# State-space block and attention on one core: input projection by channel block in 512 columns, halo rows apart, new orders, LayerNorm shift from PSUM

## The chip, the cores and the metric

The program runs on one core of a Trainium2 chip. Its engines work side by side, each through its own queue in order: PE (TensorE, matmuls and transposes), ACT (ScalarE), DVE (VectorE), POOL (GpSimd), and SP, which issues the DMAs. They wait for each other through semaphores. The metric is the device time of one execution in microseconds, the median of several; lower is better.

## The reference

Input x is (4, 64, 64, 256) in fp32. Layer 0, cut to its lines:

```python
x_norm = _layernorm(x, norm_g, norm_b)
xz = x_norm @ in_proj_W                       # 256 -> 2 x 384
x_proj, z = (xz[..., :INNER], xz[..., INNER:])
windows = _window_partition(x_proj, WS)       # 2 x 2 windows: sequences of 4 tokens
y_fwd = _light_s6(windows, fwd_...)           # proj; dt = silu(..); state = exp(dt*a)*state + dt*b*x; y = state.c
y_bwd = jnp.flip(_light_s6(jnp.flip(windows, 1), bwd_...), 1)     # 8 states per channel and direction
y_ssm = _window_unpartition(0.5 * (y_fwd + y_bwd), WS, h, w, b)
y_dw = depthwise 3x3 convolution of x_proj, padding 'SAME'
y_conv = jax.nn.gelu(y_dw @ pw_W, approximate=False)
y = alpha * y_ssm + (1.0 - alpha) * y_conv
x_out = shortcut + y * jax.nn.silu(z) @ out_W
h2 = _layernorm(x_out, norm2_g, norm2_b)
return x_out + jax.nn.gelu(h2 @ fuse_W1 + fuse_b1, approximate=False) @ fuse_W2 + fuse_b2
```

Layer 1 is self-attention over the 4096 pixels of each image, with 32-channel queries and keys. The change doesn't touch it.

## The kernel before, in words

Layer 0 goes over 32 tiles of 512 tokens (8 image rows of 64). A tile k has a front (LayerNorm, input projection, dt, x by token, the gates), a middle (16 chains, 8 states in 2 directions, over 4 tokens) and a back (mixing, output projection, second LayerNorm, fuse, keys, queries and values for layer 1). An iteration of the loop runs the middle of tile k, the back of k - 1 (steps with `-`), the front of k + 1 (steps with `+`), and conv, pw and z of tile k. The order on each engine is written out by hand in `PE_ORDER`, `ACT_ORDER`, `DVE_ORDER` and `POOL_ORDER`. Steps that the prediction names:

- `xnt0/1`, `xnth`: PE turns the normalized x to channels first; `xnth` turns the two halo rows (above and below the tile). `xnt` holds for each half (dr, even or odd rows) 256 tokens and 64 halo columns.
- `inx0` to `inx5`: input projection of channel block cb = i // 2 and half dr = i % 2: 2 matmuls of 320 columns (L489; each matmul is two passes in the profile, each with a weight load), then three copies on ACT: `x_ch` (L686), the padded image `xp` (L691), and the halo row of xp (L694).
- `proj`, `dtf0` to `dtf3`, `dtb0` to `dtb3`: dt of token t, forward and backward; a pair is issued together in the `dtb` step (L534, L538) and copied by ACT with silu (L717) to `dt`. `xk0` to `xk2`: x by token, `x_win` (L733). `bct`: gates b and c.
- `argq` (POOL, L828) multiplies dt with the rates of chain q; `expq` (ACT, L782, L783) takes its exponents; `stN` (DVE) is a third of a slot of the recurrence; `accq` (POOL, L841) adds the chain's last output; `umf`/`umb` (POOL, L819) make u = dt * x_win.
- `yt`, `out0/1`, `ln2_stats/mean/std/shift/norm`, `h2t`, `w10` to `w21`, `x1t0/1`, `fg0` (keys and queries), `v0/1` (values): the back. `ln2_shift` and `ln1_shift` are L880, -mean / std for 4 or 5 rows of tokens.
- `conv0a` waits for conv's bank and input; the 108 small matmuls are issued in `conv2a`, `conv0b` and `conv2c`. `z0` to `z2` project the gate. `ow` scales two tokens of y.

Results of front steps go in turn through three PSUM banks (`psF`, `BANK_OF`), those of the back through two (`psB`), states through three (`psS`, columns 0 to 383). A PE step waits until the former user of its bank is copied. ACT loads a table (L651, 1.28 us) when it changes between exp, silu and gelu: ten times in a tile.

SP waits for `w21` and stores the residual; then waits for `fg0`, stores keys and queries in six DMAs, loads the next `xb` in four, and stores the values behind `v0` and `v1`.

## Time and profile before

| what | value |
|---|---|
| median of 3 runs | 4567.81 us (4566.51 to 4570.78) |
| profiled execution | 4575.34 us |
| its span on the core | 4573.5 us |
| granted TensorE clock over the span | 0.983 |
| layer 0 (about 0 to 2612 us), layer 1 (2612 to the end) | 32 tiles; 32 chunks of queries |

Times in the rows are microseconds from the start of the span. A timeline row has: start, length (of all that it merges), engine, line, operation, out<-in with shapes, count, and in brackets the engine's idle time before it and who ended it. The length of one instruction includes a tail that overlaps the next instruction on its engine, so the pace is read from starts. PEclk is the granted clock as a share of full speed. An engine whose idle time is short is near its limit, but what bounds a loop of engines is the chain that has no spare wait in it.

### The profile page before, as it was taken

What the parts mean: (1) busy time and instruction counts of PE and PEld (TensorE: products, weight loads), DVE (VectorE), ACT (ScalarE), POOL (GpSimd) and SP (SyncE); (2) the same over time, 40 slices, a digit from 0 to 9 for tenths busy, and PEclk for the clock granted to TensorE, in tenths of its full rate; (3) what the DMA queues carried; (4) which work ended last, traced back from release to release, by engine and by line L of the source; (5) the groups of instructions that cost most, each with busy time, mean ns of one, the idle gap of its engine ahead of it and who ended that gap; (6) DMA issues with size and microseconds to landing.
All of it is one profiled execution on the core that took longest, in us unless ns stands there. A gap on an engine that the chain in (4) does not pass through costs nothing. (4 is left out here: it accounts for less than half of the span.)

```text
span 4573.5 us, 78801 instructions
## 1 busy us (share of the span) xinstructions
...
## 2 busy tenths in 40 slices
...
DMA packets 139073, 194.82 MB, mean 43 GB/s; under 512 B 18428, under 2 KB 106470, under 8 KB 138726
## 3 DMA queue, kind: packets, MB, share of 16 engines
...
q8 instruction: 166, 2.72, 0.2%
...
## 5 line engine op out<-in xcount | busy, mean ns | idle before, releaser
L1423 POOL TENSOR_TENSOR pl<-probs,ph 128x512 fp32r<-128x512 f32 x1024 | 1318.7, 1289 | 543.9 <-PE ps_o L1527 269.0
L828 POOL TENSOR_TENSOR dec<-dt,rates 128x384 f32<-128x384 f32 x1536 | 1493.1, 1003 | 253.9 <-ACT dt L717 198.3
L1626 ACT ACTIVATE ph<-ps_s 128x512 fp32r<-128x512 f32 x1024 | 613.3, 599 | 773.3 <-PE ps_s L1510 768.7
L1639 DVE TENSOR_REDUCE part_max<-ps_m 128x1 f32<-128x512 f32 x992 | 667.3, 688 | 343.8 <-PE ps_m L1495 343.5
L1519 PE MATMUL ps_o<-ph,values_high 128*128 128x512 f32 x2048 | 809.1, 395 | 0.1
L1519 PE MATMUL ps_o<-ph,values_low 128*128 128x512 f32 x2048 | 804.4, 393 | 0.0
L1669 DVE TENSOR_TENSOR ps_a<-probs,ps_a 128x512 f32<-128x512 f32 x992 | 682.1, 688 | 48.0 <-ACT probs L1628 40.4
L1527 PE MATMUL ps_o<-pl,values_high 128*128 128x512 f32 x2048 | 634.4, 391 | 0.0
L1628 ACT ACTIVATE probs<-ps_s 128x512 f32<-128x512 f32 x1024 | 609.5, 595 | 0.0
L986 DVE SCALAR_TENSOR_TENSOR psS<-u,bc,psS 128x384 f32<-128x384 f32 x1024 | 597.1, 615 | 1.2
L995 DVE SCALAR_TENSOR_TENSOR y_tok<-psS,bc,y_tok 128x384 f32<-128x384 f32 x960 | 554.7, 608 | 4.5
L841 POOL TENSOR_TENSOR y_tok<-y_tok,dec 128x384 f32<-128x384 f32 x512 | 512.5, 1001 | 20.1 <-DVE dec L976 14.0
L782 ACT ACTIVATE psS<-dec 128x384 f32<-128x384 f32 x512 | 256.1, 500 | 351.8 <-POOL dec L828 327.4
L962 DVE SCALAR_TENSOR_TENSOR psS<-u,bc,psS 128x384 f32<-128x384 f32 x512 | 314.0, 613 | 202.2 <-ACT psS L782 200.3
L489 PE MATMUL psF<-xnt,in_w 128*128 128x320 f32 (+1 forms) x1152 | 438.2, 510 | 14.7 <-ACT xp L694 12.5
L1519 PEld LDWEIGHTS ps_o<-ph,values_high 128*128 128x128 f32 x2048 | 388.2, 190 | 92.1 <-DVE o_ch L1674 0.5
L1519 PEld LDWEIGHTS ps_o<-ph,values_low 128*128 128x128 f32 x2048 | 388.1, 190 | 86.1
L1527 PEld LDWEIGHTS ps_o<-pl,values_high 128*128 128x128 f32 x2048 | 384.9, 188 | 87.3
L783 ACT ACTIVATE dec<-dec 128x768 f32<-128x768 f32 x512 | 428.8, 838 | 0.0
L651 ACT ACT_TABLE_LOAD x319 | 409.3, 1283 | 5.6
L489 PEld LDWEIGHTS psF<-xnt,in_w 128*128 128x128 f32 x1152 | 218.7, 199 | 177.9 <-issue 114.3
L510 PE MATMUL psF<-xp,conv_w 32*32 32x512 f32 x6912 | 269.8, 594 | 32.1 <-ACT q_sb L722 32.1
...
## 6 DMA issues: line engine op xcount, KB each, us to landing
...
xf<-in_x_dram SPq DMA_DIRECT2D x128, 128.0 KB
xb<-in_x_dram SPq DMA_DIRECT2D x128, 128.0 KB
...
out_dram<-res SPq DMA_DIRECT2D x128, 128.0 KB
```

Of the source, the lines that this page charges most:

```text
L489: mm = pe.matmul(outs, wts[:, kb, :], src[:, kb], start=kb == 0, stop=kb == KB - 1)
L828: last = nc.gpsimd.tensor_tensor(dec[:, q % RING, j - 1, :], dt[:, par, d, token_of(d, j), :], rates[:, d, n, :], ALU.mult)
L841: nc.gpsimd.tensor_tensor(y_tok[:, par, t, :], y_tok[:, par, t, :], dec[:, q % RING, T - 2, :], ALU.add).then_inc(acc_ok, 1)
L986: nc.vector.scalar_tensor_tensor(s_t, u[:, d, t, :], scalar(q, t, "b"), s_t, ALU.mult, ALU.add).then_inc(state_ok, 1)
L995: nc.vector.scalar_tensor_tensor(y_t, s_t, scalar(q, t, "c"), y_t, ALU.mult, ALU.add).then_inc(state_ok, 1)
L1423: nc.gpsimd.tensor_tensor(pl[:, m % DEPTH, :], probs[:, m % DEPTH, :], ph[:, m % DEPTH, :].bitcast(F32), ALU.subtract).then_inc(pl_ok, 1)
L1519: mm = pe.matmul(ps_o[cb][:, :], v[:, m, cb * P:(cb + 1) * P], ph[:, m % DEPTH, :], start=m == 0 and v is vh, stop=False)
L1527: pe.matmul(ps_o[cb][:, :], vh[:, m, cb * P:(cb + 1) * P], pl[:, m % DEPTH, :], start=False, stop=m == KEYS - 1).then_inc(lo_done[cb], 1)
L1626: nc.scalar.activation(ph[:, m % DEPTH, :], ps_s[m % 2][:, :], ACT.Exp).then_inc(ph_ok, 1)
L1628: nc.scalar.activation(probs[:, m % DEPTH, :], ps_s[m % 2][:, :], ACT.Exp).then_inc(probs_ok, 1)
L1639: nc.vector.tensor_reduce(part_max[:, qt, kc:kc + 1], ps_m[r % 2][:, :], AX.X, ALU.max).then_inc(max_out, 1)
L1669: nc.vector.tensor_tensor(ps_a[:, :], probs[:, m % DEPTH, :], ps_a[:, :], ALU.add).then_inc(acc_ok, 1)
```

## The change

The input projection of x is done by whole channel block: `inx0` to `inx2`, each 2 matmuls of 512 columns, one `x_ch` copy and two `xp` copies. The lower halo row of the three blocks is one step `inh` with 6 matmuls of 64 columns (two per block) and three copies; the upper halo row is copied by ACT from the last row of the tile before, which lies in the other half of `xp`, in one instruction for the three blocks. The orders are new. `ln1_shift` and `ln2_shift` copy the mean into unused columns of a state bank in PSUM, wait for that copy, and read it from there. With 29 front jobs in place of 32, banks go round by three throughout.

```diff
 PE_ORDER = """
-    z0 z1 yt0- yt1- yt2- z2 out0- conv0a out1- conv1a conv2a conv0b conv0c conv1c conv2c xnt0+ h2t0- h2t1- xnt1+
+    z0 z1 yt0- yt1- yt2- z2 out0- out1- conv0a conv1a conv2a conv0b conv0c conv1c conv2c xnt0+ h2t0- h2t1- xnt1+ pw0
...
-BANK_OF = {step: (i % FRONT_BANKS if i < len(FRONT_JOBS) - len(FRONT_JOBS) % FRONT_BANKS else 1)
-           for i, step in enumerate(jobs(True, (0, 1), True))}
+BANK_OF = {step: i % FRONT_BANKS for i, step in enumerate(jobs(True, (0, 1), True))}
...
+                if job == "inh":
+                    for cb in range(CB):
+                        for kb in range(KB):
+                            mm = pe.matmul(bank[:, cb * W:(cb + 1) * W], in_w[:, kb, cb * P:(cb + 1) * P],
+                                           xnt[:, kb, 1, TOK // 2:], start=kb == 0, stop=kb == KB - 1)
...
-                    if kind == "inx":
-                        cb, dr = int(i) // 2, int(i) % 2
-                        outs, src = bank[:, 0:TOK // 2 + W], xnt[:, :, dr, :]
-                        wts = in_w[:, :, cb * P:(cb + 1) * P]
...
+                    outs = bank[:, :].rearrange("p (h n) -> p h n", h=2)
+                    src = xnt[:, :, :, 0:TOK // 2]
+                    c0 = (INNER if kind == "z" else 0) + int(i or 0) * P
+                    wts = xproj_w if kind == "proj" else in_w[:, :, c0:c0 + P]
...
                 elif kind == "v":
+                    if i == 0:
+                        pe.wait_ge(back_act, emptied(g, "x1t1")[1])
...
-                    cb, dr = int(job[-1]) // 2, int(job[-1]) % 2
-                    nc.scalar.activation(x_ch[:, cb, dr * 256:(dr + 1) * 256], bank[:, 0:TOK // 2], ACT.Identity,
+                    cb = int(job[-1])
+                    nc.scalar.activation(x_ch[:, cb, :], bank[:, :], ACT.Identity,
                                          scale=mix[:, 0, cb:cb + 1], bias=mixed_bias[:, cb:cb + 1])
...
+                    for dr in range(2):
+                        dst = xp[:, par, cb, 1 + dr:dr + ROWS:2, 1:W + 1].rearrange("p wr (wc dc) -> p dc wr wc", dc=2)
+                        last = nc.scalar.activation(dst, bank[:, dr * 256:(dr + 1) * 256].rearrange(
+                            "p (dc wr wc) -> p dc wr wc", dc=2, wr=ROWS // 2), ACT.Identity, bias=in_bias[:, cb:cb + 1])
+                elif job == "inh":
+                    if not (exact(f) and f == 0):
+                        act.wait_ge(front_out, front_job(f - 1, "inx2"))
+                    nc.scalar.activation(xp[:, par, :, 0, 1:W + 1], xp[:, 1 - par, :, ROWS, 1:W + 1], ACT.Copy,
+                                         scale=edge[:, bass.ds(2 * f, 1)])
+                    for cb in range(CB):
+                        last = nc.scalar.activation(xp[:, par, cb, ROWS + 1, 1:W + 1], bank[:, cb * W:(cb + 1) * W],
+                                                    ACT.Identity, scale=edge[:, bass.ds(2 * f + 1, 1)],
+                                                    bias=halo_bias[:, cb, bass.ds(2 * f + 1, 1)])
...
                     dve.wait_ge(ok, base + 2)
+                    mean = mv[:, :, 0:1]
+                    if own_bank is not None:
+                        mean = own_bank[:, INNER:INNER + n].rearrange("p (t s) -> p t s", s=1)
+                        nc.vector.tensor_copy(mean, mv[:, :, 0:1]).then_inc(mean_ok, 1)
+                        means.append(tile)
+                        dve.wait_ge(mean_ok, len(means))
                     dve.wait_ge(std_ok, tile + 1)
-                    last = nc.vector.scalar_tensor_tensor(shift[:, :, :], mv[:, :, 0:1], -1.0, std[:, :, :],
+                    last = nc.vector.scalar_tensor_tensor(shift[:, :, :], mean, -1.0, std[:, :, :],
```

In the order tables, ACT has `z2` ahead of `ln1_norm` and `xnth` ahead of `w10`; `fg0` stands behind the `xk` steps on PE and ACT and behind `st47` on DVE, `v0` where it stood; on DVE `out0`, `out1` and `ln2_shift` stand one `st` step earlier each; on POOL `acc0` and `acc5` change places with `umb0` and `umb3`, and `acc14` stands ahead of `umf3`.

PE from the second dt pair to the keys, queries and values; dt_w is the pair, xb the turns `x1t0` and `x1t1`, fg_w `fg0`, y_ch `xk`, value_w `v0`. Before:

```order
L534 MATMUL psF<-dt_w,proj_sb 128x384 x2
L538 MATMUL psF<-bias_row,two 128x384 x2
L489 MATMUL psF<-xnt,in_w 128x320 x2
L456 MATMUL psB<-ident,xb 128x128 x4
L534 MATMUL psF<-dt_w,proj_sb 128x384 x2
L538 MATMUL psF<-bias_row,two 128x384 x2
L456 MATMUL psB<-ident,xb 128x128 x4
L489 MATMUL psF<-xnt,in_w 128x320 x2
L534 MATMUL psF<-dt_w,proj_sb 128x384 x2
L538 MATMUL psF<-bias_row,two 128x384 x2
L609 MATMUL psB<-xt,fg_w 64x512 x2
L456 MATMUL psF<-ident,y_ch 128x128 x12
```

And now:

```order
L533 MATMUL psF<-dt_w,proj_sb 128x384 x2
L537 MATMUL psF<-bias_row,two 128x384 x2
L455 MATMUL psB<-ident,xb 128x128 x4
L533 MATMUL psF<-dt_w,proj_sb 128x384 x2
L537 MATMUL psF<-bias_row,two 128x384 x2
L470 MATMUL psF<-xnt,in_w 128x64 x6
L455 MATMUL psB<-ident,xb 128x128 x4
L533 MATMUL psF<-dt_w,proj_sb 128x384 x2
L537 MATMUL psF<-bias_row,two 128x384 x2
L616 MATMUL psB<-value_w,xt 128x256 x4
L455 MATMUL psF<-ident,y_ch 128x128 x12
L608 MATMUL psB<-xt,fg_w 64x512 x2
```

The projection between the first two dt pairs is gone, the one ahead of the last pair has become `inh` and stands ahead of `x1t1`, and `fg0` has changed places with `v0`.

ACT in the same place, from the second dt pair's copies on (y_ch is x_ch here, xt the copies of `x1t`). Before:

```order
L717 ACTIVATE dt<-psF 128x384 x2
L686 ACTIVATE y_ch<-psF,mixed_bias,mix 128x256
L691 ACTIVATE xp<-psF,in_bias 128x2x4x32
L694 ACTIVATE xp<-psF,halo_bias,edge 128x64
L766 ACTIVATE xt<-psB 128x512
L717 ACTIVATE dt<-psF 128x384 x2
L766 ACTIVATE xt<-psB 128x512
L686 ACTIVATE y_ch<-psF,mixed_bias,mix 128x256
L691 ACTIVATE xp<-psF,in_bias 128x2x4x32
L694 ACTIVATE xp<-psF,halo_bias,edge 128x64
L717 ACTIVATE dt<-psF 128x384 x2
```

And now:

```order
L724 ACTIVATE dt<-psF 128x384 x2
L773 ACTIVATE xt<-psB 128x512
L724 ACTIVATE dt<-psF 128x384 x2
L698 ACTIVATE xp<-xp,edge 128x3x64
L701 ACTIVATE xp<-psF,halo_bias,edge 128x64 x3
L773 ACTIVATE xt<-psB 128x512
```

Two half jobs of three copies each have gone from here, and the four copies of `inh` stand ahead of the second `xt` copy; the third dt pair's copies follow.

## Rows read from the trace of the kernel before

**Rows 1.** Windows: stretch, busy us (count) by engine, PEclk, DMA share, GB/s.
```profile
69.30:2406.70 2337.40, 2183.41 (x14206) 1375.58 (x14207) 2131.49 (x4364) 1905.41 (x3404) 2094.66 (x2161) 0.98 0.12 40
1236.75:1313.92 77.17, 72.73 (x481) 46.07 (x480) 71.28 (x147) 63.76 (x116) 69.83 (x73) 1.00 0.13 44
1313.92:1392.65 78.73, 74.37 (x481) 46.87 (x480) 71.28 (x147) 63.87 (x116) 69.84 (x73) 0.98 0.12 41
```
**Rows 2.** Source L660: duration ns min/median/max, first and last start us.
```profile
L660 ACT ACTIVATE std<-mv,eps x31: 283/284/288, 69.3 to 2406.7; 128x5 f32<-128x5 f32 x31
```
**Rows 3.** Windows ahead of and at the lower clock, second tile.
```profile
1370.00:1373.00 3.00, 1.43 (x10) 0.96 (x11) 3.00 (x7) 2.99 (x8) 1.90 (x2) 1.00 0.30 123
1373.10:1376.00 2.90, 2.90 (x8) 1.53 (x8) 1.88 (x4) 1.70 (x5) 0.00 (x0) 0.50 0.01 3
```
**Rows 4.** Timeline of PE: start us, length us, op, tiles, count.
```profile
1295.90 1.24 PE L489 MATMUL psF<-xnt,in_w 128*128 128x320 f32 x4
...
1373.11 2.34 PE L489 MATMUL psF<-xnt,in_w 128*128 128x320 f32 x4
```
**Rows 5.** Timeline of ACT in the tile from 1236.70.
```profile
1255.36 2.08 ACT L750 ACTIVATE hid<-xb,shift,std 128x256 f32<-128x256 f32 x4 [1.95 <-DVE shift L880]
...
1264.64 0.49 ACT L782 ACTIVATE psS<-dec 128x384 f32<-128x384 f32 x1 [0.99 <-POOL dec L828]
...
1273.63 0.49 ACT L782 ACTIVATE psS<-dec 128x384 f32<-128x384 f32 x1 [0.77 <-POOL dec L828]
...
1276.70 0.56 ACT L686 ACTIVATE y_ch<-psF,mixed_bias,mix 128x256 f32<-128x256 f32 x1
1277.14 0.51 ACT L691 ACTIVATE xp<-psF,in_bias 128x256 f32<-128x256 f32 x1
1277.52 0.41 ACT L694 ACTIVATE xp<-psF,halo_bias,edge 128x64 f32<-128x64 f32 x1
1277.80 0.71 ACT L763 ACTIVATE hid<-psB,col 128x512 f32<-128x512 f32 x1
...
1293.37 0.87 ACT L717 ACTIVATE dt<-psF 128x384 f32<-128x384 f32 x2
...
1295.70 0.91 ACT L717 ACTIVATE dt<-psF 128x384 f32<-128x384 f32 x2
...
1298.29 0.88 ACT L717 ACTIVATE dt<-psF 128x384 f32<-128x384 f32 x2
...
1302.22 1.54 ACT L733 ACTIVATE x_win<-psF 128x512 f32<-128x512 f32 x3
```
**Rows 6.** Timeline of POOL in the same tile.
```profile
1256.52 1.00 POOL L841 TENSOR_TENSOR y_tok<-y_tok,dec 128x384 f32<-128x384 f32 x1 [0.26 <-DVE dec L976]
...
1298.87 2.92 POOL L828 TENSOR_TENSOR dec<-dt,rates 128x384 f32<-128x384 f32 x3 [4.01 <-ACT dt L717]
...
1303.88 3.87 POOL L819 TENSOR_TENSOR u<-dt,x_win 128x384 f32<-128x384 f32 x4 [1.13 <-ACT x_win L733]
```
**Rows 7.** Timeline of PE in the same tile.
```profile
1248.31 8.35 PE L510 MATMUL psF<-xp,conv_w 32*32 32x512 f32 x216 [0.59 <-ACT q_sb L722]
1258.02 0.66 PE L456 MATMUL psF<-ident,xf 128*128 128x128 f32 x4 [1.36 <-ACT y_ch L707]
...
1290.96 1.34 PE L489 MATMUL psF<-xnt,in_w 128*128 128x320 f32 x4 [0.26 <-ACT xp L694]
...
1294.38 0.88 PE L534 MATMUL psF<-dt_w,proj_sb 48*128 48x384 f32 x3 [1.64 <-ACT dt L717]
...
1299.95 1.53 PE L456 MATMUL psF<-ident,y_ch 128*128 128x128 f32 x12
```
**Rows 8.** Timeline of DVE in the same tile.
```profile
1254.54 0.79 DVE L880 SCALAR_TENSOR_TENSOR shift<-mv,std 128x4 f32<-128x4 f32 x1
...
1301.01 0.62 DVE L962 SCALAR_TENSOR_TENSOR psS<-u,bc,psS 128x384 f32<-128x384 f32 x1 [3.21 <-ACT psS L782]
```
**Rows 9.** Source L1265, the same instruction in the setup.
```profile
L1265 DVE SCALAR_TENSOR_TENSOR shift<-mv,std x1: 166/166/166, 23.8 to 23.8; 128x5 f32<-128x5 f32 x1
```

More of the change, by code:

```diff
@@ L40 @@
 PE_ORDER = """
-    z0 z1 yt0- yt1- yt2- z2 out0- conv0a out1- conv1a conv2a conv0b conv0c conv1c conv2c xnt0+ h2t0- h2t1- xnt1+
-    pw0 w10- xnth+ pw1 w11- proj+ pw2 inx0+ w12- inx1+ w13- inx2+ dtf0+ dtb0+ w20- inx3+ w21- dtf1+ dtb1+ inx4+
-    x1t0- dtf2+ dtb2+ x1t1- inx5+ dtf3+ dtb3+ fg0- xk0+ xk1+ xk2+ v0- bct+ v1-
+    z0 z1 yt0- yt1- yt2- z2 out0- out1- conv0a conv1a conv2a conv0b conv0c conv1c conv2c xnt0+ h2t0- h2t1- xnt1+ pw0
+    w10- xnth+ pw1 w11- proj+ pw2 inx0+ w12- inx1+ w13- inx2+ dtf0+ dtb0+ w20- w21- dtf1+ dtb1+ x1t0- dtf2+ dtb2+
@@ L44 @@
+    inh+ x1t1- dtf3+ dtb3+ v0- xk0+ xk1+ xk2+ fg0- bct+ v1-
 """.split()
 ACT_ORDER = """
-    exp1 ln1_std+ exp2 ow exp3 z0 z1 ln1_norm+ z2 exp4 ln2_std- exp5 ln2_norm- conv0c conv1c conv2c xnt0+ exp6
-    h2t0- h2t1- xnt1+ exp7 exp8 pw0 w10- xnth+ pw1 w11- exp9 proj+ exp10 pw2 inx0+ w12- inx1+ w13- exp11 inx2+
-    exp12 dtf0+ dtb0+ exp13 inx3+ exp14 dtf1+ dtb1+ inx4+ x1t0- dtf2+ dtb2+ x1t1- inx5+ dtf3+ dtb3+ exp15 fg0-
-    xk0+ xk1+ xk2+ exp0+ v0- bct+ v1-
+    exp1 ln1_std+ exp2 ow exp3 z0 z1 z2 ln1_norm+ exp4 ln2_std- exp5 ln2_norm- conv0c conv1c conv2c xnt0+ exp6 h2t0-
@@ L50 @@
+    h2t1- xnt1+ exp7 exp8 pw0 xnth+ w10- pw1 w11- exp9 proj+ exp10 pw2 inx0+ w12- inx1+ w13- exp11 inx2+ exp12 dtf0+
+    dtb0+ exp13 exp14 dtf1+ dtb1+ x1t0- dtf2+ dtb2+ inh+ x1t1- dtf3+ dtb3+ exp15 v0- xk0+ xk1+ xk2+ exp0+ fg0- bct+
+    v1-
 """.split()
 DVE_ORDER = """
-    st0 ln1_stats+ st1 ln1_mean+ st2 yt0- st3 yt1- st4 st5 yt2- st6 ln1_shift+ st7 st8 st9 out0- st10
-    out1- ln2_stats- ln2_mean- st11 st12 st13 ln2_shift- st14 st15 st16 st17 st18 st19 st20 st21 st22
-    st23 st24 st25 st26 st27 st28 st29 st30 st31 st32 st33 st34 st35 st36 st37 st38 st39 w20- w21- st40 st41
@@ L55 @@
-    st42 st43 st44 st45 fg0- st46 st47 gd_mul+ v0- gd_sum+ v1-
+    st0 ln1_stats+ st1 ln1_mean+ st2 yt0- st3 yt1- st4 st5 yt2- st6 ln1_shift+ st7 st8 out0- st9 out1- st10
+    ln2_stats- st11 ln2_mean- st12 ln2_shift- st13 st14 st15 st16 st17 st18 st19 st20 st21 st22 st23 st24 st25 st26
+    st27 st28 st29 st30 st31 st32 st33 st34 st35 st36 st37 st38 st39 w20- w21- st40 st41 st42 st43 st44 st45 v0-
+    st46 st47 gd_mul+ fg0- gd_sum+ v1-
 """.split()
 POOL_ORDER = """
-    arg2 arg3 umb0 acc0 arg4 acc1 arg5 umb1 umb2 acc2 arg6 acc3 arg7 acc4 arg8 umb3 acc5 arg9 acc6 arg10 acc7
@@ L59 @@
-    arg11 acc8 arg12 acc9 arg13 acc10 arg14 acc11 arg15 acc12 arg0+ acc13 umf0+ umf1+ umf2+ umf3+ acc14 acc15
-    arg1+
+    arg2 arg3 acc0 umb0 arg4 acc1 arg5 umb1 umb2 acc2 arg6 acc3 arg7 acc4 arg8 acc5 umb3 arg9 acc6 arg10 acc7 arg11
+    acc8 arg12 acc9 arg13 acc10 arg14 acc11 arg15 acc12 arg0+ acc13 umf0+ umf1+ umf2+ acc14 umf3+ acc15 arg1+
 """.split()
@@ L458, in front @@
             def front(step, f, par):
-                kind, i = (step, "") if step in ("proj", "bct", "xnth") else (step[:-1], step[-1])
+                kind, i = (step, "") if step in ("proj", "bct", "xnth", "inh") else (step[:-1], step[-1])
                 job = step
```

35 lines of the change are left out of this document (14 added, 21 removed).

## The prediction

> **What bounds the kernel now.** The page has PE busiest, but it adds up two layers, and the change touches layer 0 alone. A window over layer 0, from 69.3 to 2406.7, has PE busy 2183 of 2337 us, DVE 2131, POOL 2095, ACT 1905 [rows 1]: four engines nearly full, so the sums don't name the bound. `std<-mv,eps` (step `ln1_std`) runs once a tile, 31 times from 69.3 to 2406.7 [rows 2]: a tile takes 2337.4/30 = 77.91 us on average.
>
> Two neighbouring tiles differ: 77.17 us at a granted clock of 1.00, then 78.73 us at 0.98 [rows 1]. A window in the second shows PEclk 0.50, the lower level (1.2 GHz); just before, PE had worked 1.43 us in 3.00 [rows 3]. Four passes of L489 that take 1.24 us in the first tile, at 1295.90, take 2.34 there [rows 4]. So a thin stretch of PE around `dtf2` costs 1.56 us in some tiles, and the mean gives their share: (77.91 - 77.17)/1.56 = 0.47.
>
> Then the timeline of the tile at full clock, 1236.70 to 1313.87 (all times below are in it), engine by engine, for what each waits for last.
> - ACT waits for POOL's exponents at 1264.64 (0.99) and last at 1273.63 (0.77, `exp10`). From there until it has copied `x_win` (three copies from 1302.22) its rows have no wait [rows 5].
> - POOL waits for ACT at 1298.87 (4.01, for `dt`) and at 1303.88 (1.13, for `x_win`). From there until `exp10`'s exponents of the next tile it waits once, 0.26 for DVE, at 1256.52 [rows 6].
>
> These two pieces close a loop: ACT from 1273.63 to 1303.88 is 30.25 us, POOL from 1303.88 to 1273.63 + 77.17 is 46.92; together 77.17, the whole period. PE's waits (0.59, 1.36, 1.64) are for ACT [rows 7], and DVE has 3.21 us spare at 1301.01 [rows 8]. So the bound is ACT's in-order queue from `exp10` to `xk2`, and POOL's 47 us behind it, and not PE.
>
> **The change, part by part.**
>
> *Input projection on ACT.* An `inx` job now goes from 1276.70 to 1277.80: 0.44 for the x_ch copy, 0.38 for xp, 0.28 for the halo, 1.10 in all, six times 6.60 [rows 5]. After: three jobs of one 512-column copy with scale and bias and two xp copies. The 512 columns cost between 0.48 (L733, plain, the pace of three in 1.54 with the tail off) and 0.88 (twice 0.44); I take the middle, 0.67. Three jobs: 3 x (0.67 + 0.76) = 4.29. `inh` adds three halo copies at 0.28 and one of 3 x 64 from SBUF, between 0.28 and 0.44, taken as 0.40: 1.24. Sum 5.53, **1.07 us less** for ACT in the loop (ends 0.3 and 1.7).
>
> *Input projection on PE.* Six times 1.24 = 7.44 now. By columns 3 x 512 stand against 6 x 320: 5.95. The 6 matmuls of 64 columns have 12 passes with a weight load each; nearest are the 12 turns of L456 at 1299.95, 1.53 us [rows 7]; by columns alone they would be 0.5. With 1.5 PE's work stays the same; the edit can pay only through ACT.
>
> *How much of ACT's saving arrives.* Up to `dtf1` there are four half jobs now (4.40) and three full ones after (4.29): 0.1 us; `exp13` and `exp14` now stand together, and the table loads are as many. So dtf1's copy starts near 1293.2 (now 1293.37). PE's 1.64 us wait to 1294.38 ends when both copies are done; after the change `dtf2` and `dtb2` lie in the banks of `dtb0` and `dtf1`, and PE can start near 1293.8. By its rows PE then needs about 1.1 us for the pair, 1.4 for `inh`, 0.5 for `x1t1`, 1.1 for the next pair: ready at 1294.9, 1296.2, 1296.7 and 1297.8. ACT waits for it: dtf2/dtb2 to 1295.7 (two copies, some 0.8), `inh` 1296.2 to 1297.5, `x1t1` to 1298.0, then dtf3, whose copy now starts at 1298.29 [rows 5]. That is 0.3 us earlier, and 0.6 if the 512 columns take less than I count. `v0` stands ahead of `xk0` where `fg0` was, one 512-column copy for another. I take **0.55 us** for the loop (ends 0 and 1.2).
>
> *POOL.* `acc14` ahead of `umf3` moves one addition; nothing is added. It delays DVE's `st0` of the next tile, which needs all four u, by one addition at most, and DVE comes to `st0` only behind `st47`, `gd_mul`, `fg0`, `gd_sum` and `v1`. The 0.26 wait at 1256.52 should go, since DVE's queue gets there sooner (next two items): **0.2 us** (ends 0 and 0.26).
>
> *LayerNorm shift.* L880 on 4 elements takes 0.79 us; the same instruction on 5 elements took 0.166 in the setup (L1265), before POOL's loop ran [rows 8, 9]. After: a copy to PSUM and a product from it, at 0.166 each with a wait between, about 0.4. Twice a tile DVE saves 0.4; if either waits as L880 does, nothing. The Trainium skill ("SBUF — State Buffer", two separate sides) has a pair of ports that GpSimd and a Vector instruction with two SBUF inputs take in turn, each for its whole length; by that rule one input in PSUM frees L880, and the 0.166 agrees. Either way it lies beside DVE's 3.21 us.
>
> *`out1` ahead of `conv0a`, `z2` ahead of `ln1_norm`.* PE's wait at 1248.31 (0.59) goes, and the one before `out1`. `ln2_shift` stands one piece of `states` earlier, about 1 us, so `ln2_norm` can start about 1.1 us before 1255.36, and with it the conv copies and PE's 1258.02. The wait of 1.36 there stays, as conv ends that much earlier too. What is late next: ACT meets POOL's exponents at 1264.64, and will wait 2.1 in place of 0.99. **Nothing**, with POOL's pace as the cover; without it, 1.1 us.
>
> *SP.* `fg0` is emptied some 4 us later on DVE, and behind it on SP stand six stores of keys and queries, four `xb` loads and the two v stores. `xb` is read by `out0`, behind `st8` of the next tile; no wait of now is for it, and I count nothing (upper end: 1 us a tile, in rival 2).
>
> At full clock: 77.17 - 0.55 - 0.2 = 76.42.
>
> **The clock.** Now PE runs `inx4` at 1290.96 after a wait of 0.26, `x1t0`, then idles 1.64 [rows 7]: 1.9 us idle. After, `inx4` is gone. dtf1/dtb1 end near 1290.8, `x1t0` waits for DVE's `w21`, which stands where it stood, until about 1292.1, and PE idles again until 1293.8: about 2.5 us idle. So I expect the lower clock in more tiles, 0.7 of them (ends: 0.2, as a shorter period shifts where tiles fall, and 1). Its price stays at 1.56, since it falls on dtf2, `inh` and dtf3, for which ACT waits.
>
> A mean tile: 76.42 + 0.7 x 1.56 = 77.51, 0.40 less than 77.91; times 31 tiles, **12 us**. The profiled execution took 4575.3, 1.8 more than its span and 7.5 more than the median of the runs shown; against that median, 4567.8, the forecast is **4555**.
>
> **Rivals.**
> 1. *The lower clock in every tile.* 76.42 + 1.56 = 77.98, 2 us slower in all: 4570. For it: 2.5 us idle in place of 1.9. Against: half of the tiles with 1.9 kept the full clock. The Trainium skill ("TensorE: Matmul & The Clock Gate", what's actually happening) says that the low level is the default and activity lifts it; by that rule thinning this stretch counts against the change. Chance 0.15.
> 2. *Slower: `inh` is too long.* It stands ahead of `x1t1` and `dtf3` with a turn of its own on PE and four copies on ACT, where ACT already waits for PE. If it costs ACT 0.8 us more than I count, the loop gains nothing, and that is where this case begins to decide. At 1.2 more: 77.4 at full clock, with 0.9 of the tiles slowed 78.8, 0.9 x 31 = 28 us slower: 4596; 4580 halfway. Against: no 64-column copy exceeds 0.41. Chance 0.13.
> 3. *The thin stretch costs less often*: share 0.2. 76.42 + 0.31 = 76.73, 1.18 x 31 = 37 us: 4531. For it: the share now rests on where a tile's 1.9 us fall, and the period changes that. Chance 0.22.
> 4. *POOL's pace holds*: no gain in the loop, share as now: 4568. Against: POOL waits 4.01 and 1.13 for ACT. Chance 0.08.
>
> The forecast, share 0.5 to 0.9 and 0.4 to 1.4 off the full-clock tile, gives 4543 to 4563: chance 0.42.
>
> **Numbers.** 0.2% (9 us) is about what a measurement of this kernel can tell from no change. Faster: rival 3 (0.22) and most of the forecast (0.36): 0.58. Same: the rest of it, rival 4, and most of rival 1: 0.25. Slower: rival 2 and a little of rival 1: 0.17. The range 4525 to 4577 reaches to rivals 3 and 1; the likeliest case's own is 4543 to 4563.
>
> **What would show it.** `std<-mv,eps` about 76.4 us apart in tiles at full clock; ACT's wait for POOL at `exp8` near 2 us; a copy and a product of some 0.16 each for the shift; no wait ahead of conv; PEclk below 1.00 in about 20 of 30 tiles, near dtf2. It is wrong if full-clock tiles still take 77.2 (the loop was another one), or if the count of slowed tiles is far from 20.

## The result

| | before | after |
|---|---|---|
| median, runs on the same chip | 4569.30 us (4566.51 to 4572.12) | 4612.41 us (4611.31 to 4613.47) |
| span of the profiled execution | 4573.5 us | 4609.6 us |
| granted clock over the span | 0.983 | 0.963 |

The change makes the kernel slower: the ratio after to before is 1.0093, 95% interval 1.0081 to 1.0105. The forecast was 4555, with 4577 as its upper end.

The windows of the kernel after, over layer 0 and over one tile, answer to [rows 1] (stretch, then busy us and count of PE, PE's weight loads, DVE, ACT and POOL, then the granted clock, the DMA share and GB/s).

```profile
72.60:2439.90 2367.30, 2250.21 (x14200) 1402.90 (x14201) 2107.10 (x4422) 1870.42 (x3254) 2094.13 (x2161) 0.94 0.12 39
1254.96:1333.59 78.63, 75.55 (x480) 47.23 (x479) 70.43 (x149) 62.54 (x110) 69.84 (x73) 0.96 0.12 40
```

The step `ln1_std` and the two instructions of the shift, each by its source line (duration in ns), answer to [rows 2, 9].

```profile
L661 ACT ACTIVATE std<-mv,eps x31: 282/284/286, 72.6 to 2439.9; 128x5 f32<-128x5 f32 x31
...
L895 DVE SCALAR_TENSOR_TENSOR shift<-psS,std x62: 160/164/166, 77.7 to 2537.3; 128x5 f32<-128x5 f32 x31, 128x4 f32<-128x4 f32 x31
...
L891 DVE COPY psS<-mv x62: 153/157/159, 77.5 to 2537.1; 128x5 f32<-128x5 f32 x31, 128x4 f32<-128x4 f32 x31
```

A tile takes (2439.9 - 72.6)/30 = 78.91 us against 77.91, so 1.00 x 30 = 30 of the 36 us are in the loop. DVE, ACT and POOL are busy for less time or as much as before; PE alone is busy for longer, 2250 us against 2183 [rows 1], at a lower clock: PEclk 0.94 against 0.98. The trace's record of the granted clock has 28 of the 29 tiles behind the first at the lower level for a while (14 before), 222 us in all (48 before), and always from around `dtf2` and `inh` on. This is PE there (start, length, line, operation, out<-in, count, idle time ahead):

```profile
1308.19 0.92 PE L533 MATMUL psF<-dt_w,proj_sb 48*128 48x384 f32 x4
...
1310.58 0.63 PE L455 MATMUL psB<-ident,xb 128*128 128x128 f32 x4 [1.29 <-DVE xb L946]
1311.91 0.88 PE L533 MATMUL psF<-dt_w,proj_sb 48*128 48x384 f32 x3 [0.71 <-ACT dt L724]
...
1312.94 2.51 PE L470 MATMUL psF<-xnt,in_w 128*128 128x64 f32 x12
1315.24 1.06 PE L455 MATMUL psB<-ident,xb 128*128 128x128 f32 x4
1316.23 1.65 PE L533 MATMUL psF<-dt_w,proj_sb 48*128 48x384 f32 x4
...
1318.13 2.97 PE L616 MATMUL psB<-value_w,xt 128*128 128x256 f32 x8
```

and the windows of PE ahead of and inside the stretch:

```profile
1308.00:1311.50 3.50, 1.91 (x12) 0.91 (x10) 3.50 (x8) 3.47 (x6) 3.36 (x5) 1.00 0.07 27
...
1311.50:1312.90 1.40, 0.98 (x6) 0.55 (x6) 1.40 (x3) 1.14 (x3) 0.96 (x2) 1.00 0.75 307
1312.90:1315.20 2.30, 2.30 (x14) 2.27 (x13) 2.30 (x6) 0.87 (x2) 0.78 (x1) 0.59 0.01 4
...
1316.20:1322.00 5.80, 5.80 (x25) 4.21 (x25) 1.46 (x3) 4.84 (x10) 3.19 (x4) 0.66 0.00 0
```

The projection `inx4` is gone from ahead of `x1t0`, which waits 1.29 us for DVE (`w21`); `dtf2` waits 0.71 for ScalarE's dt copies. The clock is full until 1312.90 and falls right behind the start of `inh`: the window from 1312.90 to 1315.20, which `inh` fills, has 0.59, and the trace's record of the clock has the lower level (1.2 GHz) from 1313.31 to 1320.14. So what drew it in this tile stands ahead of `inh`, but for its first 0.37 us: the two idles, with the thin work around them, four turns of 128 columns and a dt pair of 48 rows. In 23 of the 28 tiles the fall lies inside `inh`'s twelve passes. All that follows is slow: `inh` takes 2.51, `x1t1` 1.06, and the four passes of the dt pair 1.65 where those of the pair ahead took 0.92 at 1308.19.

ACT and POOL of the same tile, and of the only tile behind the first that ran wholly at the full clock (229.28 to 306.37), answer to [rows 5, 6]. First ACT:

```profile
266.54 0.49 ACT L789 ACTIVATE psS<-dec 128x384 f32<-128x384 f32 x1 [0.59 <-POOL dec L835]
...
287.81 0.87 ACT L724 ACTIVATE dt<-psF 128x384 f32<-128x384 f32 x2 [0.40 <-PE psF L537]
289.29 0.46 ACT L698 ACTIVATE xp<-xp,edge 128x192 f32<-128x192 f32 x1 [0.61 <-PE psF L470]
...
1282.97 0.49 ACT L789 ACTIVATE psS<-dec 128x384 f32<-128x384 f32 x1 [1.77 <-POOL dec L835]
...
1294.84 0.77 ACT L687 ACTIVATE y_ch<-psF,mixed_bias,mix 128x512 f32<-128x512 f32 x1
1295.50 0.89 ACT L693 ACTIVATE xp<-psF,in_bias 128x256 f32<-128x256 f32 x2
...
1313.04 0.87 ACT L724 ACTIVATE dt<-psF 128x384 f32<-128x384 f32 x2 [0.40 <-PE psF L537]
1315.48 0.46 ACT L698 ACTIVATE xp<-xp,edge 128x192 f32<-128x192 f32 x1 [1.57 <-PE psF L470]
1315.85 0.98 ACT L701 ACTIVATE xp<-psF,halo_bias,edge 128x64 f32<-128x64 f32 x3
1316.72 0.60 ACT L773 ACTIVATE xt<-psB 128x512 f32<-128x512 f32 x1
1318.24 0.87 ACT L724 ACTIVATE dt<-psF 128x384 f32<-128x384 f32 x2 [0.93 <-PE psF L537]
```

Then POOL:

```profile
291.58 2.92 POOL L835 TENSOR_TENSOR dec<-dt,rates 128x384 f32<-128x384 f32 x3 [3.13 <-ACT dt L724]
...
296.54 2.93 POOL L826 TENSOR_TENSOR u<-dt,x_win 128x384 f32<-128x384 f32 x3 [1.08 <-ACT x_win L740]
...
1318.81 2.92 POOL L835 TENSOR_TENSOR dec<-dt,rates 128x384 f32<-128x384 f32 x3 [5.13 <-ACT dt L724]
...
1323.76 2.93 POOL L826 TENSOR_TENSOR u<-dt,x_win 128x384 f32<-128x384 f32 x3 [1.07 <-ACT x_win L740]
```

POOL waits 3.13 us for `dt` in the full-clock tile and 5.13 in the slowed one: there the lower clock reaches the loop. ACT's waits for PE ahead of `inh` and of the last dt pair are 1.57 and 0.93 there; at full clock the first is 0.61 and the second doesn't appear.

### The profile page after: what moved, and what is told of

Same layout as the page of the kernel before. It is cut to its first block and busy times, and to the rows that moved or that the text cites. A ratio compares the mean times of both kernels' runs of the same rounds, so it can differ in the third digit from the quotient of the medians.

```text
span 4609.6 us, 78766 instructions
## 1 busy us (share of the span) xinstructions
PE 4416.4 (96%) x24000; PEld 3128.3 (68%) x24000; DVE 3727.3 (81%) x7231; ACT 3158.7 (69%) x5620; POOL 3650.5 (79%) x3475
## 3 DMA queue, kind: packets, MB, share of 16 engines
q8 instruction: 166, 2.72, 0.2%
## 5 line engine op out<-in xcount | busy, mean ns | idle before, releaser
L835 POOL TENSOR_TENSOR dec<-dt,rates 128x384 f32<-128x384 f32 x1536 | 1493.4, 1004 | 265.7 <-ACT dt L724 219.5
L848 POOL TENSOR_TENSOR y_tok<-y_tok,dec 128x384 f32<-128x384 f32 x512 | 514.4, 1005 | 41.7 <-DVE dec L991 37.3
L488 PE MATMUL psF<-xnt,in_w 128*128 128x512 f32 x768 | 356.6, 594 | 0.9 <-ACT bc L710 0.7
L997 DVE TENSOR_TENSOR psS<-psS,dec 128x384 f32<-128x384 f32 x512 | 283.3, 553 | 1.1
L826 POOL TENSOR_TENSOR u<-dt,x_win 128x384 f32<-128x384 f32 x256 | 253.5, 1008 | 38.3 <-ACT x_win L740 38.3
```

Source lines behind the costliest of these rows:

```text
L835: last = nc.gpsimd.tensor_tensor(dec[:, q % RING, j - 1, :], dt[:, par, d, token_of(d, j), :], rates[:, d, n, :], ALU.mult)
L848: nc.gpsimd.tensor_tensor(y_tok[:, par, t, :], y_tok[:, par, t, :], dec[:, q % RING, T - 2, :], ALU.add).then_inc(acc_ok, 1)
```

## The experiments

In the kernels with fill in their name PE runs extra matmuls into a bank that is free at that moment, and nobody reads their results: they take away idle time of PE and put wide work in its place. Each measured time is a median; the ratio behind it, with its 95% interval, is to the kernel before run beside it (medians of 4569.3 to 4572.6 us, so a difference of two kernels that were not run together is good to some 3 us). Slowed tiles are counted behind the first, 29 in all; in the first the clock is low for 34 to 44 us in every kernel.

### Is it the clock, and is it the idle time?

**after_fill**: the kernel after, with extra matmuls in both idles.

```diff
+            def busy_work(bank, widths, free, n):
+                pe.wait_ge(free, n)
+                for cols in widths:
+                    pe.matmul(bank[:, 0:cols], w1[:, 0, 0:P], w1[:, 1, 0:cols], start=True, stop=True)
...
+                    if part == "all" and step == "x1t0":
+                        busy_work(psF[front_bank(tile, "dtf2")], (512, 256), front_out, bank_user_before(k + 1, "dtf2")[0])
+                    if part == "all" and step == "dtf2":
+                        busy_work(psB[BACK_JOBS.index("x1t1") % BACK_BANKS], (384,), back_dve, emptied(k - 1, "w21")[1])
```

> The changed kernel plus matmuls whose result nobody reads, where PE stands idle: 512 and 256 columns ahead of x1t0, 384 ahead of dtf2. Theory A (the loss is TensorE's lower clock, drawn by the thin stretch there, with tiles of 77.1 us at full clock): PEclk 1.00 in nearly all tiles, a mean tile of 77.1 to 77.3 in place of 78.9, so 50 us less than the changed kernel, about 4560. Theory B (the loss is the path of inh through PE and ACT): the added work can only cost, 4612 or more.

Measured: 4523.84 us, ratio 0.9892 (0.9875 to 0.9908). More work, and 89 us less than the kernel after, where 50 were expected. PE in the same stretch, the extra matmuls being L623:

```profile
1270.19 1.56 PE L623 MATMUL psF<-w 128*128 128x512 f32 x4
1271.59 0.60 PE L455 MATMUL psB<-ident,xb 128*128 128x128 f32 x4
1272.02 0.81 PE L623 MATMUL psB<-w 128*128 128x384 f32 x2
1272.90 0.88 PE L533 MATMUL psF<-dt_w,proj_sb 48*128 48x384 f32 x3
...
1273.92 1.55 PE L470 MATMUL psF<-xnt,in_w 128*128 128x64 f32 x12
...
1277.48 1.97 PE L616 MATMUL psB<-value_w,xt 128*128 128x256 f32 x8 [0.55 <-ACT xt L782]
```

`inh` takes 1.55 in place of 2.51, no tile behind the first is slowed, and a tile takes 76.19 us on average. So the lower clock costs the kernel after 78.91 - 76.19 = 2.72 us a tile, 82 us in 30. The 77.1 that the expectation took for a full-clock tile was too long: the one such tile stands behind a slowed one.

**after_fill_gap1** (only the first `busy_work`) and **after_fill_gap2** (only the second) ask which idle it is.

> The changed kernel with only the first filler, 512 and 256 columns in the 1.29 us wait ahead of x1t0; the 0.71 us ahead of dtf2 stays empty. Theory A1 (it is the sum of idle time and thin work around dtf2 that draws the lower clock, and 0.7 us idle is less than the 1.36 us that never drew it elsewhere): full clock in nearly all tiles, 4524 to 4532. Theory A2 (thin work by itself is enough: x1t0, dt with 48 rows, inh with 64 columns, x1t1): slowed tiles remain, 4550 or more.

> The changed kernel with only the second filler, 384 columns in the 0.71 us ahead of dtf2; 1.29 us stay idle ahead of x1t0. The first filler alone gave 4528. Theory A1 (idle time summed over the stretch decides; 1.29 is less than the 1.36 that draws nothing ahead of xnt0): full clock mostly, 4525 to 4545. Theory A2 (thin work counts as little as none, so 1.29 idle between it is too much): slowed tiles in half or more, 4560 or more.

Measured: 4527.71 (0.9898; 0.9881 to 0.9914) and 4529.4 (0.9907; 0.9890 to 0.9923), no slowed tile in either. Either idle alone (0.70 or 1.29 us) leaves the full clock; the two together don't. The extra matmuls are wide work as well as less idle time, and these runs don't tell the two apart.

**before_fill**: the same in the kernel before, 512 and 384 columns ahead of `dtf2`.

> The kernel before with matmuls of 512 and 384 columns, read by nobody, in the 1.64 us wait ahead of dtf2. Theory A: the 14 slowed tiles of 78.7 become 77.2, 22 us less than before, about 4547, PEclk 1.00 over layer 0. Theory B says nothing of the clock: 4568 or more, since work is added.

Measured: 4549.80 (0.9950; 0.9933 to 0.9966), tiles of 77.20, none slowed. The kernel before, too, pays (77.91 - 77.20) x 30 = 21 us for its clock.

**before_thin**: the kernel before with `inx4` ahead of `dtf1` on PE and ACT, which takes away the work between `dtb1` and `x1t0` as the change does; on ACT its copies now stand ahead of `dtf1`'s.

```diff
-    dtf0+ dtb0+ w20- inx3+ w21- dtf1+ dtb1+ inx4+ x1t0- dtf2+ dtb2+ x1t1- inx5+ dtf3+ dtb3+
+    dtf0+ dtb0+ w20- inx3+ w21- inx4+ dtf1+ dtb1+ x1t0- dtf2+ dtb2+ x1t1- inx5+ dtf3+ dtb3+
```

> The kernel before with nothing changed but inx4's place on PE and ACT: ahead of dtf1 in place of behind dtb1, so that x1t0's stretch is as empty as in the changed kernel. Theory A: the share of slowed tiles goes from 0.47 to 0.8 or more, 4585 to 4610. Theory B (clock follows from inh, or from nothing in this stretch): within 8 us of before.

Measured: 4644.18 (1.0157; 1.0140 to 1.0173), every tile slowed, where 4585 to 4610 was expected. One moved step in the old kernel costs 73 us. PE there:

```profile
1328.72 0.66 PE L456 MATMUL psB<-ident,xb 128*128 128x128 f32 x4
1331.77 1.65 PE L534 MATMUL psF<-dt_w,proj_sb 48*128 48x384 f32 x4 [2.39 <-ACT dt L717]
...
1334.58 2.34 PE L489 MATMUL psF<-xnt,in_w 128*128 128x320 f32 x4
```

The wait ahead of `dtf2` is 2.39 us, and `inx5` takes the 2.34 of [rows 4] behind it. Not all of the 73 us is clock: behind the first two, its tiles alternate between about 79.5 us with 3.4 at the lower level and 80.9 with 6.8. By that slope a tile without it would take some 78.1 (an estimate), 0.9 over before_fill's 77.20. That part would be the move itself; no run of this kernel with extra matmuls shows it.

### Which part of the change does what

**proj_only**: the new projection alone, its jobs at the places of the old ones (`inx1` where `inx2` stood, `inx2` where `inx4` stood, `inh` where `inx5` stood), mean from SBUF. **proj_fill**: the same with 512 extra columns ahead of `dtf2`.

```diff
-    inx0+ w12- inx1+ w13- inx2+ dtf0+ dtb0+ w20- inx3+ w21- dtf1+ dtb1+ inx4+ x1t0- dtf2+ dtb2+ x1t1- inx5+ dtf3+
+    inx0+ w12- w13- inx1+ dtf0+ dtb0+ w20- w21- dtf1+ dtb1+ inx2+ x1t0- dtf2+ dtb2+ x1t1- inh+ dtf3+
```

> The new projection under the orders of before (inx1 and inx3 dropped, inx2 and inx4 become full jobs, inx5 becomes inh), mean from SBUF, no filler; with filler it took 4534 with tiles of 76.42. Theory A: one full job stands in the thin stretch, but the wait for dtf1's copy is longer and inh's thin work follows it; slowed tiles in half or more, each 1.5 to 2.3: 4560 to 4590. Theory D (the projection never draws the clock; the new orders did): 4534 to 4545.

> The new projection alone: orders of before with inx1, inx3 dropped, inx2 and inx4 become the second and third full job, inx5 becomes inh; mean from SBUF; a filler of 512 columns ahead of dtf2. To be read against before with filler, 4550 (tiles of 77.19). The step of the prediction (ACT's shorter copies shorten the loop by 0.55): tiles of 76.6, 4533. If the gain of the changed kernel came from orders and shift: 4548 to 4552. If inh blocks ACT: above 4555.

Measured: 4531.87 (0.9913; 0.9896 to 0.9929) and 4533.90 (0.9915; 0.9898 to 0.9931), both with tiles of 76.49 and none slowed. The projection alone is worth 77.20 - 76.49 = 0.71 us a tile at full clock, and it takes away the slowed tiles of before as well: the full job `inx2` stands ahead of `x1t0`, and the one idle left ahead of `dtf2` is 1.16. ACT, which comes sooner now, has a wait for POOL at `exp14` that the kernel before doesn't have:

```profile
1273.09 0.49 ACT L789 ACTIVATE psS<-dec 128x384 f32<-128x384 f32 x1 [0.46 <-POOL dec L835]
```

**before_psum** and **before_psum_fill**: the kernel before with the mean through PSUM, without and with the extra matmuls of before_fill.

> The kernel before with the mean copied to PSUM, no filler; with filler it took 4546, tiles of 76.87, against 77.19. Tiles at full clock of 76.9; the share of slowed tiles decides the rest: 0.47 as now gives 4560; 0.3 to 0.9 gives 4552 to 4580. If it comes out above 4572, a part of the changed kernel that only shortens DVE is a loss through the clock alone.

> The kernel before with the mean copied to PSUM and the filler ahead of dtf2, against before with filler alone, 4550. Theory C1, as predicted: DVE is shorter by 0.8 us a tile and nothing else moves, 4548 to 4552. Theory C2: the 0.26 us wait of POOL for DVE goes and later waits with it, 0.2 to 0.5 us a tile, 4534 to 4544.

Measured: 4570.80 (0.9999; 0.9989 to 1.0009) and 4546.05 (0.9938; 0.9921 to 0.9954). At full clock a tile is 0.30 shorter (76.90 against 77.20); without the extra matmuls 17 tiles are slowed in place of 14, and the gain is gone.

**after_sbuf**: the kernel after with the mean read from SBUF (`if False:` in place of `if own_bank is not None:`), and **after_sbuf_fill**, with both `busy_work` calls as well.

> The changed kernel with the LayerNorm mean read from SBUF again, no copy to PSUM. Theory A and B both: DVE has over 2 us spare a tile, so the time stays within 5 us of the changed kernel's 4612; L895's shift takes 0.79 us again. Theory C (DVE's queue is now in the loop, as POOL waits for it at acc0, 0.7 us): about 0.4 us a tile more, 4622 or more.

> The changed kernel with both fillers and the mean read from SBUF again, so that the shift is priced without the lower clock around dtf2. Theory C1 (the shift lies beside DVE's spare time at full clock; its 27 us were all clock): within 5 us of the 4524 with the shift from PSUM. Theory C2 (DVE's queue sets POOL's and ACT's waits in the new orders): full-clock tiles of 76.5 to 77.3 in place of 76.14, 4536 to 4560.

Measured: 4638.96 (1.0145; 1.0128 to 1.0162) and 4649.18 (1.0167; 1.0150 to 1.0184). The first fits only the third theory, and the second is 89 us or more above both. In the new orders the PSUM copy is worth 27 us, and 125 in the filled kernels. Rows of the filled one show how. DVE:

```profile
1282.11 3.38 DVE L904 SCALAR_TENSOR_TENSOR shift<-mv,std 128x5 f32<-128x5 f32 x1
...
1295.40 0.62 DVE L904 SCALAR_TENSOR_TENSOR shift<-mv,std 128x4 f32<-128x4 f32 x1
```

POOL at the same time:

```profile
1281.61 0.99 POOL L835 TENSOR_TENSOR u<-dt,x_win 128x384 f32<-128x384 f32 x1
1282.57 2.90 POOL L844 TENSOR_TENSOR dec<-dt,rates 128x384 f32<-128x384 f32 x3
1287.74 1.00 POOL L857 TENSOR_TENSOR y_tok<-y_tok,dec 128x384 f32<-128x384 f32 x1 [2.27 <-DVE dec L1000]
```

and PE behind it:

```profile
1298.73 1.11 PE L455 MATMUL psF<-ident,xf 128*128 128x128 f32 x4 [3.60 <-ACT y_ch L723]
```

`ln1_shift` from SBUF takes 3.38 us and ends just as POOL's four back-to-back products (from 1281.61 to 1285.47) do; POOL itself then waits 2.27 for DVE, `ln2` is late, and PE idles 3.60 ahead of `xnt0`. Every tile falls to the lower clock behind that idle, and the extra matmuls around `dtf2` can't help. How much of the 125 us is this clock and how much the delay itself wasn't separated. With the mean in PSUM the same instruction takes 160 to 166 ns in all of its 62 runs. The Trainium skill ("SBUF — State Buffer", two separate sides) says that of a GpSimd instruction and a Vector instruction with two SBUF inputs, the one that starts first holds a shared pair of ports for its whole length, and the other waits. The trace agrees that the product with two SBUF inputs waits and the one with an input in PSUM doesn't; but the wait here covered POOL's whole run of instructions, not one. A run doesn't always shut it out: `ln2_shift`, in the middle of three back-to-back products (1295.00 to 1297.91), is through in 0.62. And in after_sbuf `ln1_shift` takes 0.15 or 0.16 in 18 of its 31 runs, as at 402.12, where it starts just as POOL goes from one instruction to the next, and 3.25 to 4.48 in 12:

```profile
402.12 0.16 DVE L895 SCALAR_TENSOR_TENSOR shift<-mv,std 128x5 f32<-128x5 f32 x1
```

So where the product meets POOL decides; what lets it in stays open.

**proj_psum**: projection and PSUM copy, all in the old orders.

> The kernel before with the new input projection and the PSUM copy of the mean, everything else in the old places, and no added matmuls. Theory A (the new orders let the lower clock in, the two other parts are gains that add up): full-clock tiles of 76.42 less about 0.3, that is 76.1, no tile slowed, since the thin stretch keeps its one idle of about 1.2 us; about 4523 us. Rival (part of the 76.14 of the filled kernel after belongs to the new orders): 76.4 and 4530 us. A second rival: the earlier end of the LayerNorm gives the stretch ahead of the delta weights another wait, and some tiles fall to the lower clock: 4535 to 4560.

Measured: 4525.90 (0.9898; 0.9881 to 0.9914), no slowed tile, 76.24 on average. Two parts of the change alone give what the filled kernel after gives (4523.84), without extra matmuls.

### Which move of the orders

**after_inx2_late**: `inx2` behind `dtb1` on PE and ACT. **after_inh_late**: `inh` (the halo matmuls; its expectation below calls them a transpose) behind `dtb3` on both.

```diff
-    inx0+ w12- inx1+ w13- inx2+ dtf0+ dtb0+ w20- w21- dtf1+ dtb1+ x1t0- dtf2+ dtb2+ inh+ x1t1- dtf3+ dtb3+
+    inx0+ w12- inx1+ w13- dtf0+ dtb0+ w20- w21- dtf1+ dtb1+ inx2+ x1t0- dtf2+ dtb2+ inh+ x1t1- dtf3+ dtb3+
...
+    inx0+ w12- inx1+ w13- inx2+ dtf0+ dtb0+ w20- w21- dtf1+ dtb1+ x1t0- dtf2+ dtb2+ x1t1- dtf3+ dtb3+ inh+
```

> The changed kernel with inx2 moved on PE and ACT from ahead of dtf0 to behind dtb1: 1.7 us of the kernel's own work in the thin stretch. Theory A: fewer tiles at the lower clock (under 20 of 30) and for a shorter time in each, a mean tile near 77.7, 4570 to 4585. Theory B: inh is where it was, so no more than 10 us change from 4612, or slower, as inx2's copies now stand ahead of dtf2's on ACT.

> The kernel after with only the transpose of the current tile's inh moved back behind the transposes of B, on TensorE and ScalarE, so that less thin work stands between the two idles. Theory A (the lower clock is drawn by idle time and thin work together, and inh's matmuls with their 0.4 to 0.6 us of wait make the stretch twice as long as before): the low spell is short again and in fewer tiles, 4570 to 4595 us. Rival (only the two idles of 1.3 and 0.7 us count): 27 or more of 30 tiles slowed as before, 4605 to 4620 us. Rival that ends lower still: with inh gone the second idle is closed too, no slow tile, 4525 us.

Measured: 4600.89 (1.0065; 1.0049 to 1.0082), 21 tiles slowed, and 4600.62 (1.0061; 1.0045 to 1.0078), 15 slowed but for some 10 us each (154 us in all). Each gives back only 12 us; the idles of 1.28 and 0.71 stay in the second, and in the first 0.84 and 0.72. after_inx2_late comes nearest to theory B. For after_inh_late no expectation was right: fewer slowed tiles, with longer stays.

**after_stretch_old**: all moves from `inx0` to `v1` taken back on PE, ACT and DVE, the other moves kept. **proj_psum_stretch_new**: the converse, only those moves made in proj_psum.

> The kernel after, with the input projection's jobs, inh, fg0 and v0 back in their old places on TensorE, ScalarE and VectorE (everything from inx0 to v1), the other moves of the new orders (out1, z2, xnth, ln2_shift, the additions and umb/umf on GpSimd) kept. Theory A (the stretch around dtf2 alone lets the lower clock in, the other moves are neutral): no slowed tile, full-clock tiles of 76.1 to 76.2, 4520 to 4530 us. Rival (another of the moves, such as the earlier ln2_shift or acc0 ahead of umb0, makes or shares the cause): part or all of the loss stays, 4560 to 4612 us.

> The converse: the new projection and the PSUM copy in the old orders, with only the part from inx0 to v1 of the new orders on TensorE, ScalarE and VectorE. Theory A: the whole loss of the kernel after, 25 or more of 30 tiles slowed, 4600 to 4620 us. Rival (the other moves are needed too): between 4526 and 4590 us.

Measured: 4540.17 (0.9929; 0.9912 to 0.9945) and 4619.51 (1.0101; 1.0085 to 1.0118). From both sides the stretch holds the loss: 72 us gained where it is undone, 94 lost where it alone is done, with 21 tiles slowed (25 or more were expected). But 12 tiles of after_stretch_old are still slowed, behind one idle of 1.53, where none was expected. Of its others, those behind a full-clock tile take 75.6 us, less than in any kernel so far; those behind a slowed one take some 76.2.

**after_stretch_old_fill** (512 extra columns ahead of `dtf2`) and **after_stretch_inh_first** (no extra matmuls, `inh` moved ahead of `dtf2` on PE and ACT) go on from there.

> The kernel with the new projection, the PSUM copy and the new orders outside the stretch (full-clock tiles of 75.60, 13 of 30 tiles slowed, 4540 us), plus one matmul of 512 columns, whose result nobody reads, in its idle of 1.5 us ahead of dtf2. Theory A (idle and thin work there draw the lower clock, and cost nothing else): all tiles at 75.6, about 4508 us. Rival (the filler only moves the low clock elsewhere, or delays dtf2): 4525 or more.

> The same kernel without a filler, inh moved ahead of dtf2 on TensorE and ScalarE, so that real work stands in the idle. Theory A: the idle ahead of inh shrinks to about 1.1 us, as it waits for one dt copy and not two, near the 1.16 at which the kernel with the projection alone kept the full clock; dtf2 comes 1 us later, dtf3 at the same time; no slowed tile, 75.6 to 76.0, 4508 to 4522 us. Rival (ScalarE is held by the four copies of inh ahead of the dt copies, so the loop grows): full-clock tiles of 76.3 or more, 4530. Second rival (thin work brought forward counts as idle does): still ten or more slowed tiles, 4535 to 4560.

Measured: 4512.45 (0.9868; 0.9852 to 0.9885), all tiles at 75.67 on average, the fastest of all; and 4557.09 (0.9964; 0.9952 to 0.9977), 19 tiles slowed and 76.6 to 76.7 at full clock. Real work in the idle didn't do: two idles are left, with the thin `inh` between them, and at full clock the loop is 1.0 longer:

```profile
1287.19 1.55 PE L470 MATMUL psF<-xnt,in_w 128*128 128x64 f32 x12 [1.05 <-ACT dt L724]
1289.10 1.31 PE L533 MATMUL psF<-dt_w,proj_sb 48*128 48x384 f32 x4 [0.35 <-ACT xp L693]
```

The last 0.57 us, from proj_psum's 76.24 to 75.67, are nearly all on POOL: from its first `u` of a tile to its last addition ahead of the wait for `dt` it needs 1274.07 - 1207.39 = 66.68 in proj_psum and 1264.31 - 1198.15 = 66.16 in after_stretch_old_fill. In proj_psum `acc0` (L848) stands between `umb0` (L826) and the next chain's product (L835):

```profile
1207.39 3.88 POOL L826 TENSOR_TENSOR u<-dt,x_win 128x384 f32<-128x384 f32 x4 [1.15 <-ACT x_win L740]
...
1221.91 1.00 POOL L826 TENSOR_TENSOR u<-dt,x_win 128x384 f32<-128x384 f32 x1
1222.87 1.00 POOL L848 TENSOR_TENSOR y_tok<-y_tok,dec 128x384 f32<-128x384 f32 x1
1224.02 2.92 POOL L835 TENSOR_TENSOR dec<-dt,rates 128x384 f32<-128x384 f32 x3
...
1274.07 1.01 POOL L848 TENSOR_TENSOR y_tok<-y_tok,dec 128x384 f32<-128x384 f32 x1
```

In after_stretch_old_fill, with POOL's new order, `acc0` (L855) comes first, then `umb0` (L833), then the product (L842):

```profile
1198.15 2.91 POOL L833 TENSOR_TENSOR u<-dt,x_win 128x384 f32<-128x384 f32 x3 [1.13 <-ACT x_win L747]
...
1212.53 1.00 POOL L855 TENSOR_TENSOR y_tok<-y_tok,dec 128x384 f32<-128x384 f32 x1
1213.48 1.01 POOL L833 TENSOR_TENSOR u<-dt,x_win 128x384 f32<-128x384 f32 x1
1214.44 2.93 POOL L842 TENSOR_TENSOR dec<-dt,rates 128x384 f32<-128x384 f32 x3
...
1264.31 1.01 POOL L855 TENSOR_TENSOR y_tok<-y_tok,dec 128x384 f32<-128x384 f32 x1
```

From the first of the pair to the product it is 2.11 us in the old order and 1.91 in the new: a product right behind an addition starts 1.15 after it (but for the one behind `acc15`, 0.95), and nearly all other pairs of POOL's instructions follow each other in 0.96. The new order takes away two such places (`acc0`, `acc5`), 0.2 each, and with `acc14` ahead of `umf3` the first six instructions take 1203.90 - 1198.15 = 5.75 in place of 1213.27 - 1207.39 = 5.88. No run moves the additions alone, so this rests on the rows.

## Why the prediction was wrong, step by step

Tile by tile the means add up (30 tiles):

| step | us a tile | from |
|---|---|---|
| before, filled | 77.20 | before_fill |
| new projection | -0.71 | proj_only |
| mean through PSUM | -0.25 | proj_psum |
| orders outside the stretch | -0.57 | after_stretch_old_fill |
| orders from `inx0` to `v1` | +0.52 | after_fill |
| lower clock of after | +2.72 | after |
| after | 78.91 | |

The clock of before is +0.71 on 77.20.

- **The bound** was right for the kernel before: ACT's queue from `exp10` to the last `x_win`, then POOL. In proj_psum the same cut gives 1283.54 - 1254.03 = 29.51 and 46.65, in sum the 76.16 of that tile; before they were 30.25 and 46.92. But ACT now waits 0.46 us for POOL at `exp14`, so what ACT saves ahead of it doesn't all count any more.
- **Input projection on ACT, and how much of it arrives**: forecast 1.07 and 0.55; measured 0.71 a tile with the projection alone (the 1.07 less the wait of 0.46 at `exp14` would be 0.61). The copies cost what was counted: 0.66 for 512 columns (1294.84 to 1295.50, counted 0.67), 1.24 for the four of `inh` (1315.48 to 1316.72, counted 1.24). In the new stretch ACT then waits 0.40 and 0.61 for PE, and its piece is 296.54 - 266.54 = 30.00, against 30.25 before and 29.51 in the old orders: 0.25 arrives. That ACT would wait for PE there was foreseen; the wait was counted 0.3 too small.
- **POOL**: forecast 0.2, since the wait at `acc0` would go. It went, by the PSUM copy: POOL waits 0.25 for DVE there in before_fill and proj_only, and not in before_psum or proj_psum. The swaps of `acc0` and `acc5` were left out without a reason and `acc14`'s was put at nothing; together they are worth about 0.5 on the very engine that bounds.
- **LayerNorm shift, beside DVE's spare time, worth nothing**: wrong. It is worth 0.25 to 0.30 a tile in the old orders, which is the very wait at `acc0` that the POOL item counts, so it didn't lie beside spare time; in the new orders it is worth 27 us in all. The step took L880's 0.79 as its price wherever it stood; in the new orders the product from SBUF can take 3.38.
- **`out1` ahead of `conv0a`**: the wait ahead of conv went and ACT waits 1.77 at `exp8` (forecast 2.1, [rows 5] had 0.99): right. PE's wait of 1.36 behind conv was to stay; it is 0.87.
- **At full clock 76.42**: measured 76.19 filled, and 77.09 in the only such tile of the kernel after, which stands behind a slowed one. That the sum came so near is luck in part: the gain that arrives from the projection in its new stretch was counted too high (0.55 against 0.71 - 0.52 = 0.19) and the orders outside it too low (nothing against 0.57), while the wait at `acc0` was right (0.2 against 0.25).
- **The clock** is the step that failed. The idle was forecast roughly (1.29 ahead of `x1t0` and 0.71 ahead of `dtf2`, 2.0 measured, "about 2.5" forecast), but what it draws was not. The step put the share at 0.7 and kept the price at 1.56, sum 1.09 a tile; it was 28 of 29 tiles and 2.72 a tile. The price of 1.56 was that of a short stay at the lower level (48/14 = 3.4 us a slowed tile in before); in after it is 222/28 = 7.9 us, so that `inh`, `x1t1`, the last dt pair and the values are all slow, and POOL gets `dt` 2.0 us late (5.13 against 3.13). Rival 1 had the share right and took the same price: 4570 in place of 4612. The sign hung on the price: 76.19 + 28/29 x 1.56 is 77.7, still under the 77.91 of before. Each us at the lower level cost 0.37 us after (82/222) and 0.44 before (21/48), so the length of the stays, not only their number, had to be in the sum. By the Trainium skill ("TensorE: Matmul & The Clock Gate", what's actually happening) the low level is the default and activity lifts it, which counts against thinning this stretch; that was noted there. The trace agrees, with 28 tiles in place of 14. The chance of 0.15 was too small.
- **Rival 2** ended nearer (4596), but for another reason: in the new stretch ACT loses 0.3 us more at full clock than was counted, not 1.2. Its sum has a slip as well: 76.42 + 1.2 is 77.6, not 77.4, which would give about 4602.

What stays open: which share of tiles an idle draws down. Slowed tiles behind the first, with PE's idle between `dtb1` and `x1t1`: none with 0.70, 1.16 or 1.29; 19 with 1.05 + 0.35; 12 with 1.53; 14 with 0.26 + 1.64, and 17 with the same where only the mean is read from PSUM (before_psum); 21 with 0.84 + 0.72 + 0.25 (after_inx2_late) and with 1.04 + 0.71 (proj_psum_stretch_new); 15 and 28 with 1.29 + 0.71 (without and with `inh` between them and `x1t1`); all with 2.39 (before_thin). Much idle draws more tiles down than little, but in between the order is mixed, so the idle alone doesn't set it. Nor does it pick the tile: in the kernel after the two idles are 1.28 to 1.32 and 0.71 in slowed tiles and in the full-clock one alike, and in before the 1.64 is the same in all 29. That the kind of work between counts is likely, and not shown: no run here separates columns, rows and order. That a stay lasts longer because `inh` follows the idle wasn't shown: without it the stays were longer still.
